# Summing a graph kernel's edge weights by accumulating transfers instead of by GpSimd additions

## What is computed

```python
# layer 1: messages by relation, weighted by edge, divided by the summed edge weight
for r in range(4):
    w_r = where(edge_type == r, edge_weight, 0.0)
    total_msg += (xs @ W_rel[r] + b_rel[r]) * w_r[:, None]
agg = segment_sum(total_msg, dst) / maximum(segment_sum(edge_weight, dst), 1.0)[:, None]
h = x @ W_self + b_self + agg
# layer 3 (twice): the mean over incoming edges
agg = segment_sum(x[src], dst) / maximum(segment_sum(ones, dst), 1.0)[:, None]
```

## Time and profile before

| | |
|---|---|
| median of three runs | 346.32 us (345.88 to 346.45) |
| the profiled execution | 345.88 us |
| its span, first to last instruction | 343.6 us |
| outside the span | 2.3 us |
| TensorE busy | 336.5 us, 98% of the span |
| VectorE, ScalarE, GpSimd busy | 243.2, 87.1, 153.0 us |
| bytes moved by transfers | 22.07 MB |

### The profile page before, as it was taken

The page is one execution under the profiler, slowest core; times in us unless marked ns, Lnnn a source line. Parts: engine busy times, 40 slices in busy tenths (PEclk is TensorE's granted clock), DMA queues, the critical chain, the costliest instruction groups (busy, mean ns, idle before and its releaser), DMA issues.

```text
span 343.6 us, 4413 instructions
## 1 busy us (share of the span) xinstructions
PE 336.5 (98%) x1624; PEld 239.5 (70%) x1625; DVE 243.2 (71%) x428; ACT 87.1 (25%) x187; POOL 153.0 (45%) x122
## 2 busy tenths in 40 slices
PE   7999999999999999999999999999999999999996
PEld 3459887785478888888888888844774544474455
DVE  5899999988596898691484598786676555443543
ACT  3565664333410000000001062223352331112110
POOL 6000000461379999999936220491115440772020
PEclk9999999999999999999999999999999999999999
DMA  7100002728800000062300089942000000000003
GB/s 240 66 1 2 5 2 85 284 57 216 279 0 2 0 1 0 2 245 65 59 0 2 0 283 190 139 141 73 1 2 0 1 0 0 2 0 0 2 0 124
DMA packets 18630, 22.07 MB, mean 64 GB/s; under 512 B 2032, under 2 KB 10992, under 8 KB 18608
## 3 DMA queue, kind: packets, MB, share of 16 engines
q1 hardware_dynamic: 17936, 20.72, 21.6%
q0 software_dynamic: 240, 0.79, 0.8%
q10 hardware_dynamic: 432, 0.26, 0.2%
HBM read 20.72 MB, written 1.05 MB: 63 GB/s over the span
## 4 chain that ended last, share of the span: by engine, by line
PE 88%; DVE 8%; ACT 1%; DMA 1%; issue 1%; ACTq 0%; DVEq 0%
PE bank L1887 14%; PE bank L1736 14%; PE bank L1679 14%; PE bank L1616 8%; PE bank L1776 7%; PE bank L1843 6%; PE bank L1927 4%; PE bank L603 4%; PE bank L576 4%; PE bank L1875 4%; PE bank L600 3%; PE bank L1603 2%; PE bank L592 2%; DMA bias<-in_edge_type 1%; DVE stats L1209 1%; DVE h L1241 1%
## 5 line engine op out<-in xcount | busy, mean ns | idle before, releaser
L1051 ACT ACTIVATE columns<-mean_var,eps 128x1 f32<-128x1 f32 x16 | 4.7, 292 | 109.4 <-DVE mean_var L1210 109.3
L1736 PE MATMUL bank<-slots,wall 128*128 128x256 f32 x128 | 30.2, 380 | 0.0
L603 PE MATMUL bank<-slots 128*128 128x112 bf16 x256 | 27.8, 228 | 0.0
L907 POOL TENSOR_TENSOR slots<-slots 128x512 f32<-128x512 f32 x1 | 1.3, 1293 | 58.7 <-DMA slots<-in_L_gnn_W_rel 58.7
L1736 PEld LDWEIGHTS bank<-slots,wall 128*128 128x128 f32 x128 | 24.2, 190 | 3.2
L600 PE MATMUL bank<-slots 128*128 128x140 bf16 x128 | 26.2, 242 | 0.0
L386 DVE TENSOR_TENSOR slots<-slots 128x1792 bf16<-128x1792 bf16 (+1 forms) x27 | 25.0, 979 | 0.0
L1679 PE MATMUL bank<-slots,h_t 128*128 128x256 f32 x104 | 24.5, 380 | 0.0
L603 PEld LDWEIGHTS bank<-slots 128*128 128x128 bf16 x256 | 22.5, 103 | 2.7
L1887 PE MATMUL bank<-wall,h_t 128*128 128x512 f32 x48 | 22.4, 596 | 0.4 <-ACT slots L1160 0.4
L1679 PEld LDWEIGHTS bank<-slots,h_t 128*128 128x128 f32 x104 | 19.7, 190 | 3.1 <-issue 0.5
(11 more groups left out here) (293 smaller groups left out, 799.6 us busy)
## 6 DMA issues: line engine op xcount, KB each, us to landing
slots<-in_L_gnn_W_rel SPq DMA_DIRECT2D x4, 1024.0 KB, 9.6
spare<-in_L_gnn_W_ffn SPq DMA_DIRECT2D x1, 2048.0 KB, 8.0
slots<-in_L_gnn_W_ffn SPq DMA_DIRECT2D x1, 2048.0 KB, 9.1
slots<-in_L_gnn_Wr SPq DMA_DIRECT2D x8, 256.0 KB, 9.1
x<-in_x SPq DMA_DIRECT2D x4, 256.0 KB, 5.7
bias<-in_L_gnn_W SPq DMA_DIRECT2D x2, 512.0 KB, 5.0
slots<-in_L_gnn_W_self SPq DMA_DIRECT2D x1, 1024.0 KB, 5.3
bias<-in_L_gnn_b_rel SPq DMA_DIRECT2D x4, 256.0 KB, 8.4
```

Of the source, the lines that this page charges most:

```text
L603: ins = pe.matmul(place[:, :, 0:R, 0:WIDE].rearrange("p h r d -> p r h d"), low, wgt_hot[:, s, v, a, :, :, j], start=False, stop=False, sk ...
L1736: ins = pe.matmul(into, left[:, k, tile(p)], right[:, k, :], start=(n in (0, 2, 3, 5) and r == 0 and k == 0), stop=False, skip_group_check ...
```

## The change

`wgt_sum` and `cnt_sum` are no longer made by GpSimd's additions. GpSimd instead issues transfers from SBUF to SBUF: a plain copy of the first operand, and then transfers that add what they read to what stands at the destination (`accum_op=ALU.add`). Each waits for the one before it on the same tile. They begin after `built` at 2 and `hop_ready` at 8, ahead of and between GpSimd's four bias additions. The semaphores count 16 for each transfer in place of 1 for each addition.

```diff
             combine_rel(0)
             finish_build()
-            pool.wait_ge(rows_loaded, 16 * 6)
-            for t in range(NT):
+            pool.wait_ge(built, 2)
+            pool.wait_ge(hop_ready, 2 * NT)
+            pool.dma_start(wgt_sum[:], wall[:, 0]).then_inc(wgt_add, 16)
+            pool.dma_start(cnt_sum[:], wall[:, R, 0:2, :]).then_inc(cnt_add, 16)
+
+            def add_weights(r):
+
+                pool.wait_ge(wgt_add, 16 * r)
+                pool.dma_start(wgt_sum[:], wall[:, r], accum_op=ALU.add).then_inc(wgt_add, 16)
+
+            def bias_self(t):
+
                 pool.wait_ge(t_ready, use_of(H_REL, t) + 1)
                 pool.tensor_tensor(h[:, t, :], h[:, t, :], bself, ALU.add).then_inc(self_biased, 1)
+
+            add_weights(1)
+            pool.wait_ge(cnt_add, 16)
+            pool.dma_start(cnt_sum[:], wall[:, R, 2:4, :], accum_op=ALU.add).then_inc(cnt_add, 16)
+            pool.wait_ge(rows_loaded, 16 * 6)
+            bias_self(0)
+            add_weights(2)
+            bias_self(1)
+            pool.wait_ge(cnt_add, 32)
+            pool.dma_start(cnt_sum[:, 0, :], cnt_sum[:, 1, :], accum_op=ALU.add).then_inc(cnt_add, 16)
+            bias_self(2)
+            add_weights(3)
+            bias_self(3)
             pool.wait_ge(hop_ready, HOPS * NT)
             pool.wait_ge(node_s_ready, 3)
             combine_rel(1)
...
             combine_rel(2)
+            pool.wait_ge(wgt_add, 16 * R)
+            pool.dma_start(wgt_sum[:, 0:2, :], wgt_sum[:, 2:4, :], accum_op=ALU.add).then_inc(wgt_add, 16)
             combine_messages(0)
-            add_weights(2)
             combine_rel(3)
+            pool.wait_ge(wgt_add, 16 * (R + 1))
+            pool.dma_start(wgt_sum[:, 0, :], wgt_sum[:, 1, :], accum_op=ALU.add).then_inc(wgt_add, 16)
             combine_messages(1)
-            add_weights(3)
             combine_messages(2)
...
                 if n == 0:
-                    dve.wait_ge(wgt_add, NT * max(r, 1))
+                    dve.wait_ge(wgt_add, 16 * (r + 1))
```

More of the change, by code:

```diff
@@ L1690, in _ @@
                 if r == 2:
-                    pe.wait_ge(cnt_add, 2)
+                    pe.wait_ge(cnt_add, 48)
                     for m in range(NT):
@@ L1756, in _ @@
                 if r == 1:
-                    pe.wait_ge(wgt_add, NT * (R - 1) + 3)
+                    pe.wait_ge(wgt_add, 16 * (R + 2))
                     for m in range(NT):
```

## The result

The changed kernel takes 357.56 us (median of 4 runs, 356.60 to 358.26) against 346.14 us before (median of 4 on the same chip, 345.88 to 346.45). The ratio is 1.0328, interval 1.0302 to 1.0354: slower. The profiled execution is 357.55 us with a span of 355.3 us, 11.7 us longer than the span before.

A forecast was written before the change was run, and what follows sets the result against it. TensorE's unbroken row was taken as the bound. Span 343.6 - 0.3 gain + 7.0 stall (landing 104.0 against 97.0) = 350.3 us, with 2.3 outside it 352.6, rounded to 352; 8-in-10 range 345.5 to 358 us.

The forecast's parts named there:

- the likeliest case: TensorE waits 1 to 11 us ahead of relation 0's third product; 347 to 357 us, chance 0.56.
- What is removed: GpSimd's 17 additions, 24.9 us, lie beside TensorE's unbroken row; gain 0.3 us at most, from one wait at L1616.
- The wait and its path: Second 1 MB accumulation holds the fourth bias addition, keep_self(3), L1300, third product; 3.8 us, so landing needed by 97.0 us.
- The doubling: Accumulations read two operands, doubling their time on the transfer engines; 7.0 us added to the landing, lower bound 0.
- Sharing: SP's loads, 16.0 us from 74 to 94 us, share the engines: 7.5 in fixed parts, half the other 8.5 counted, 4.2.
- All 0: Other waits (loaded rows, first accumulation before the second bias addition, wgt_add at 64, both sum rows) cost TensorE nothing.
- The clock: TensorE's clock might fall to its lower level after a long stall; not in the sum, kept for 357 to 362 us.
- far slower: Accumulation over twice a copy, or issuing cost proportional to size: stall 11 to 16 us, 357 to 362 us; chance 0.10.
- no wait reaches TensorE: Accumulation costs no more than a copy, SP's loads give way: landing 92.8 to 97.0, time 345.6 to 346.4 us; chance 0.29.
- Faster: VectorE gains once GpSimd's 24.9 us of work beside it are gone; at best 344.7 us; chance 0.05.
- The last sentence of the prediction: Sign of failure: an accumulation into the sums lands as quickly as the 5.3 us of a load.
- the prediction's upper bound: GpSimd's issue of 1 MB might grow in proportion to 2.8 us, 2.1 more each; 2 us taken for the upper end.

The follow-up runs named there:

- experiment 3: Changed kernel with all four bias additions directly behind the two plain copies, ahead of every accumulation: 345.92 us, ratio 0.9986 to the kernel before.
- experiment 4: Changed kernel with accum_op left out, so every accumulation becomes a plain copy of the same bytes: 352.38 us, ratio 1.0182.
- experiment 7: Changed kernel with the counts' three transfers behind the third weight accumulation and SP's loads of relations 2 and 3 after the second accumulation: 353.97 us.
- experiments 5: Changed kernel with SP's two 1 MB loads (weights of relations 2 and 3) issued only after the second accumulation has landed: 355.74 us, ratio 1.0264.
- 6: Changed kernel with the three transfers of the counts moved behind the fourth bias addition, combine_rel(1) and combine_rel(2): 358.46 us, ratio 1.0371.
- experiment 1: Changed kernel with the fourth bias addition ahead of the third accumulation and its wait for the second: 352.97 us, ratio 1.0177.
- experiment 2: Changed kernel with the second bias addition ahead of the second accumulation and the fourth ahead of the third: 351.10 us, ratio 1.0148.
- experiment 8: Changed kernel with 32 useless matmuls on TensorE ahead of the third product's wait in relation 0: 355.67 us, ratio 1.0276.

## Why the prediction came out as it did

The chain of waits was as forecast, link by link; the time was 5.6 us too short (352 for 357.56), and the span 5.0 us (350.3 for 355.3). The wide range, to 358, holds the measured time by 0.4 us; the likeliest case's own range, to 357, does not. That the landing came out near was luck in part: two terms were off in opposite ways. By the prediction's own steps:

- **What is removed.** "0.3 us at most": 0.15 was seen, and experiment 3, which keeps that gain and has no stall, can't be told from before. 24.9 us of work off an engine that nobody waits for were worth nothing that can be measured.
- **The wait and its path.** `wgt_add` at 48, the fourth bias addition, `keep_self(3)`, L1300 (now L1308), the third product: right. From landing to product 4.30 us instead of 3.8, mostly since the bias addition took 1.57 us, not the 1.27 of the earlier trace rows, and the issue ahead of it, with the wait's end, 0.9 us, not 0.7.
- **The doubling.** "If that doubles its time on the transfer engines": right, by the rate, 197 GB/s beside 378. For the two weight accumulations the three quiet transfers are 4.6 + 7.0 + 7.0 = 18.6 us (the prediction's 15.9 + 5.6 = 21.5, from a load of the earlier trace rows that took 5.3 us where the copy within SBUF takes 4.6). In the chain of the changed kernel the adding is worth the 5.6 us of experiment 4, against 7.0 in the sum. The Trainium skill's sentence in "Collectives: The Full Stack", section on the fold count, said half the rate of a copy; by that rule, the trace agrees.
- **Sharing.** This term was mis-sized. The chain measured 31.55 us, so 12.9 beyond the quiet 18.6; the prediction had 2.8 + 1.4 for the counts and 4.2 for SP's loads, 8.4. It let 7.5 us of the loads pass in the fixed parts of its own transfers and halved the rest. The fixed parts were no gaps that SP's loads could fill for nothing: they grew. The first accumulation's start is some 4 us longer than on idle engines, behind SP's packets (experiment 7), and the engines' share is 1.05 from 82 us on. Bytes at their rates come near: 4.7 MB of SP's loads and 1.6 MB of copies at 378 GB/s are 16.7 us, 2.6 MB of accumulations at 197 are 13.2, in all 29.9 of the 31.55. (That is no law: the two big loads landed only behind 106 us, 22.7 and 24.8 us after their issue, so a part of their bytes moved later; and the same count is 4.1, 4.4 and 7.7 us short in experiments 5, 6 and 7.) The over-estimate of the quiet part hid most of this: the landing came at 106.03 for 104.0, 2.0 us off. The Trainium skill, "DMA: Bandwidth & Descriptors", "Issuing engines are not separate DMA queues", has GpSimd's and SP's transfers on the same 16 engines, interleaved. The trace agrees that they take time from each other (12.9 and 10.8 us for 7.0), and more strongly than the half that was taken; but the first accumulation was not interleaved at its start, as the 97.3% of SP's queue from 84 to 87 us shows.
- **"All 0".** Wrong for two of the other waits. The first accumulation landed at 94.9 us, not 91 to 93, and with VectorE's 2.09 us of L1303 behind it the second product came 1.76 us late. In the changed kernel the later wait swallows this, but it becomes the bound as soon as that one is gone (experiment 1). So does the wait for the counts (experiment 2). Both waits at 0 were right in the forecast's sum and wrong as a guide to a repair.
- **The clock.** The second failure: a term put at nothing. The prediction kept it for the rival "far slower" (0.10), as if only a stall of 11 us or more could bring it. It came with 7.4 us, and in experiment 2 with 2.46. Its 2.5 us, together with 2.4 from landing and path, and 0.15 of the gain, are the 5.0.

The rivals: *no wait reaches TensorE* fell with the trace of after, and experiment 4 shows that it would have fallen even with accumulation as cheap as a copy. *Faster* fell with experiment 3, where GpSimd does none of the additions of the sums and no stall hides a gain. *Far slower* gave the time (357 to 362 us), by the clock and not by the length of the stall. The last sentence of the prediction, that it fails if an accumulation lands as quickly as a load, was wrong too: in experiment 4 no transfer adds, a quiet one lands in 4.6 us, and TensorE still waits.

What stays open: why SP's packets came first for some 5 us and GpSimd's had nine tenths of the engines afterwards, and why the engines were busy with so few bytes from 84 to 88 us. The second is no work of the change: the kernel before has such a stretch too, from 82 to 84 us, at a share of 0.96 and 104 GB/s.

## What to carry to other kernels

Moving work off an engine that nobody waits for gains nothing by itself, and each wait that it puts into an engine's instruction stream holds back what stands behind it; issue the dependent transfers only behind the last instruction that a bounding engine waits for (experiment 3 costs nothing, the same transfers in the order of the change 11 us). When both queues are full, add up all bytes of the stretch at their rates, accumulations at half the rate, and don't count on gaps; here the sum was still 1.7 to 7.7 us short. And a stall of TensorE of a few microseconds has to be priced with the lower clock behind it, here 1.8 to 2.9 us more.

## What was not expected of the hardware

- An idle time of 2.46 us of TensorE was followed by matmuls at the lower clock (3.64 us for a product of 1.89); this cost 1.8 us, the wait of 7.36 us 2.5, and one of 3.45 us in experiment 4 2.9. So the price does not go by the length of the wait. Behind the 2.66 us ahead of the second product in experiment 8 there was no fall at all.
- An addition of VectorE with both operands in SBUF took 3.75 us instead of 0.68 in experiment 1 when it began beside GpSimd's issue of a transfer, and ended only behind the two additions that followed; the issue of a transfer and an addition behind it had it at 2.52 us in experiment 8. The Trainium skill's "SBUF — State Buffer", "Who interferes with whom", has the blocking of such an addition by a GpSimd instruction that reads SBUF; by that rule, the trace agrees, and the row adds that it can last through several instructions.
- GpSimd's issue of a 1 MB accumulation takes 0.88 us, of a plain copy 0.53 to 0.71, and of a 0.25 MB accumulation 0.88 too, so the issue does not grow with the size as the prediction's upper bound allowed.
- SP was held at its own issue: its two loads of 1 MB took 11.44 us to issue in the changed kernel, 3.03 us before.

```profile
83.50 11.44 SPq L878 DMA_DIRECT2D slots<-in_L_gnn_W_rel  x2
```
